# Moving one product and one subtraction per attention unit from GpSimd to VectorE

## The reference, cut to what matters

```python
xn = layernorm(x)                        # x: (8, 1024, 512), 8 images
q, k, v = (xn @ W.T + b, split in 16 heads of 32)
scores = where(tile_mask, q @ k.T / sqrt(32), -1e30)   # tile_mask: i % 256 >= j % 256
attn = softmax(scores) @ v
s = attn @ Wo.T + bo
g = silu(clip(xn @ sign(weights).T * scale + bias, -100, 100))
out = x + s * g
```

## Time and profile before

| | before |
|---|---|
| median of 3 runs | 1699.39 us (1696.45 to 1701.87) |
| profiled execution | 1697.66 us, span 1695.8 us |
| mean granted TensorE clock | 0.987 of full |
| TensorE busy | 1603.3 us |
| VectorE busy | 1237.8 us |
| ScalarE busy | 1203.0 us |
| GpSimd busy | 1157.7 us |

### The profile page before, as it was taken

The page is one execution under the profiler, slowest core; times in us unless marked ns, Lnnn a source line. Parts: engine busy times, 40 slices in busy tenths (PEclk is TensorE's granted clock), DMA queues, the critical chain, the costliest instruction groups (busy, mean ns, idle before and its releaser), DMA issues.

```text
span 1695.8 us, 34086 instructions
## 1 busy us (share of the span) xinstructions
PE 1603.3 (95%) x11812; PEld 681.8 (40%) x11812; DVE 1237.8 (73%) x1886; ACT 1203.0 (71%) x3057; POOL 1157.7 (68%) x1156
## 2 busy tenths in 40 slices
PE   8987999989999999998999989999999989999977
PEld 3432344433444344443444434443344434444423
DVE  7776676876767776787776967778676787667763
ACT  3475877767877777677776777866777767777752
POOL 0267657786677767775688765788657786677787
PEclk9998999999999999999999999999999999999999
DMA  7312312333124322244122532234312323222111
GB/s 208 119 39 69 76 45 58 99 78 89 48 55 100 91 62 52 70 106 85 42 58 76 118 72 51 56 80 105 85 43 64 97 74 64 51 64 70 50 53 50
DMA packets 182952, 125.97 MB, mean 74 GB/s; under 512 B 104734, under 2 KB 157214, under 8 KB 182332
## 3 DMA queue, kind: packets, MB, share of 16 engines
q1 hardware_dynamic: 182300, 123.40, 29.0%
q10 hardware_dynamic: 480, 0.39, 0.1%
HBM read 41.40 MB, written 17.02 MB: 34 GB/s over the span
## 4 chain that ended last, share of the span: by engine, by line
PE 61%; DVE 13%; issue 8%; ACT 7%; POOL 6%; SPq 3%; DMA 1%; POOLq 0%; DVEq 0%; ACTq 0%
PE pJ L568 24%; PE pO L791 11%; PE pJ L772 7%; POOL acc L1296 4%; DVE mx L1145 3%; SPq L1400 3%; PE pS L745 3%; PE pJ L768 2%; PE pJ L660 2%; ACT PT L893 2%; PE pJ L664 2%; PE pJ L661 2%; ACT pS L913 2%; PE pJ L711 2%; DVE acc L1173 2%
## 5 line engine op out<-in xcount | busy, mean ns | idle before, releaser
L893 ACT ACTIVATE PT<-pJ 128x512 f32<-128x512 f32 (+1 forms) x1080 | 608.6, 577 | 345.4 <-PE pJ L772 330.7
L1296 POOL TENSOR_TENSOR acc<-acc,PT 128x512 f32<-128x512 f32 (+1 forms) x640 | 779.5, 1256 | 24.0 <-PE pO L791 23.9
L772 PE MATMUL pJ<-QK 97*128 97x512 f16 (+3 forms) x1280 | 383.7, 319 | 7.5 <-ACT acc L893 6.6
L1145 DVE TENSOR_REDUCE mx<-pS 128x3 f32<-128x1536 f32 (+3 forms) x264 | 377.0, 1439 | 0.0
L1129 DVE TENSOR_REDUCE mx<-pS 128x1 f32<-128x384 f32 (+3 forms) x330 | 207.0, 633 | 100.7 <-PE pS L728 99.2
L1141 DVE TENSOR_REDUCE mx<-pJ 128x1 f32<-128x512 f32 (+3 forms) x264 | 151.4, 584 | 175.3 <-PE pJ L745 118.4
L791 PE MATMUL pO<-PT,V 128*32 128x512 f32 (+2 forms) x2800 | 259.4, 483 | 2.6 <-ACT PT L893 2.6
L913 ACT ACTIVATE pS<-pS,a 128x128 f32<-128x128 f32 (+1 forms) x480 | 245.8, 514 | 1.2
L568 PE MATMUL pJ<-xT,wh_q 128*128 128x512 f16 x512 | 194.0, 389 | 2.2 <-DVE xT L1107 1.8
L568 PE MATMUL pJ<-xT,wh_k 128*128 128x512 f16 x512 | 193.7, 381 | 2.0 <-DVE U L1240 2.0
L568 PE MATMUL pJ<-wh_v,xT 128*128 128x512 f16 x512 | 190.1, 380 | 1.3 <-DVE sg L1117 1.3
(11 more groups left out here) (172 smaller groups left out, 2759.4 us busy)
## 6 DMA issues: line engine op xcount, KB each, us to landing
QK<-sg SPq DMA_DIRECT2D x762, 64.0 KB, 2.0
xs<-in_x SPq DMA_DIRECT2D x60, 256.0 KB, 3.2
xr<-in_x SPq DMA_DIRECT2D x58, 256.0 KB, 3.1
out<-xr SPq DMA_DIRECT2D x58, 256.0 KB, 2.5
QK<-aT SPq DMA_DIRECT2D x256, 1.0 KB, 1.7
QK<-in_x SPq DMA_DIRECT2D x8, 256.0 KB, 3.8
rq<-moved SPq DMA_DIRECT2D x120, 2.0 KB, 1.8
QK<-in_mqk SPq DMA_DIRECT2D x2, 512.0 KB, 9.3
```

The lines of the kernel that those rows point to most:

```text
L772: ins = e.matmul(slot[:, to:to + 512 - q0], k4[0:97, j, kc], q4[0:97, j, q0:512], start=True, stop=True)
L893: e.activation(probabilities_at(i), bank("t", i)[:, 0:cols], ACT.Exp, scale=SS).then_inc(s_p, 1)
L1145: e.tensor_reduce(mx[:, par, part, :].rearrange("p (j q) -> p j q", q=4)[:, 0:3, qi], pS[:, :, c0:c0 + w], AX.X, ALU.max).then_inc(s_m0, 1)
L1296: e.tensor_tensor(a, a, PT[:, RING_AT[i] % NPT, 0:width * len(heads)].rearrange("p (j q) -> p j q", j=len(heads)), ALU.add).then_inc(s_ap, 1)
```

## The change

The product of odd units and the subtraction of all units but the last are issued by VectorE and no longer by GpSimd. The operands, the semaphores, the waits and the nominal times are the same; the two generators are handed to VectorE's in_time.

```diff
@@ vector: behind outputs() @@
+            def normalise_outputs():
+                for n in range(1, NU - 1, 2):
+                    yield past("sm", n) + TM["out"][2]
+                    ln.wait_ge(s_R, n + 1)
+                    ln.wait_ge(*outputs_taken(n))
+                    e.tensor_tensor(On[n % 2][:, :], On[n % 2][:, :], R[:, :], ALU.mult).then_inc(s_on, 1)
+            def low_outputs():
+                for n in range(NU - 1):
+                    gn, qs = divmod(n, NQS)
+                    s, cs = gn % NSLOT, slice(qs * 512, qs * 512 + 512)
+                    yield past("sm", n) + TM["hi"][1][1] if n in ADD_AT else at_pv(n, 3) + TM["hi"][1][0]
+                    ln.wait_ge(s_oh, n + 1)
+                    e.tensor_tensor(Onl[:, s, cs], On[n % 2][:, :], Onh[:, s, cs], ALU.subtract).then_inc(s_ol, 1)
...
-                    first_layer_norm(), layer_norm(), split_x(), take_xt(), stage_qk(), gates(), outputs(), last_outputs(), results(), last_results())
+                    first_layer_norm(), layer_norm(), split_x(), take_xt(), stage_qk(), gates(), outputs(), normalise_outputs(), low_outputs(), last_outputs(), results(), last_results())
@@ gpsimd @@
-            def normalise():
...
-            def low_outputs():
...
-            in_time(additions(), first_layer_norm(), layer_norm(), normalise(), low_outputs(), gates(), results())
+            in_time(additions(), first_layer_norm(), layer_norm(), gates(), results())
```

## The result

The changed kernel takes 1704.69 us (median of 9 runs, 1702.52 to 1708.08), the kernel before, run beside it, 1699.28 (9 runs, 1692.04 to 1702.03). The ratio is 1.0039 with a 95% interval of 1.0021 to 1.0056: slower by 6.6 us if the ratio is taken of 1699.28, by 5.4 by the medians. The forecast was 1706.0, slower. The profiled execution took 1702.68 us, its span is 1700.8.

What follows compares the result with a forecast made beforehand. TensorE was taken as the bound, with VectorE deciding at 955 to 976 us in each image. 6.0 + 0.5 + 2.0 - 0.4 - 1.0 = +7.1 us gave 1706.5 against the median, forecast 1706, range 1696 to 1718.

Steps and rivals of the forecast that it cites:

- the 0.76 us piece: TensorE idle ahead of L745 at 977.22, released by VectorE's maxima L1145; expected to grow by about 1 us.
- the pair: Subtractions of units 33 and 34, and their likes per image, landing ahead of VectorE's L1141 at 955.16.
- (a): Subtraction pairs 35/36, 37/38 and 39/40 land in VectorE idle time, such as 2.06 us ahead of L1141 at 1006.14: hidden.
- (b): Subtractions 33/34 entering VectorE's full stretch at 955 us: 1.0 us per image, 6.0 in six; last image 0.5.
- The holding: VectorE's two-input subtractions blocked by GpSimd's L1319 beside them: 0.4 us taken for each, between 0 and 1.07.
- The saving: L1232 at 951.99 shortens without GpSimd's subtraction beside it, so the pair begins up to 0.66 us earlier; 0.5 taken.
- (c): Products landing between VectorE's row-score maxima: 0.3 us per image for all four, 2.0 us over seven.
- (d): First image: subtraction 2 costs 0.9 us ahead of L1117; additions until 137.34 end 1.27 sooner; net -0.4 us.
- (e): GpSimd relieved elsewhere, where additions behind its subtractions mostly waited for TensorE anyway: -1.0 us for the whole kernel.
- GpSimd was the bound: Rival: shorter GpSimd queues finish the clamp sooner, so ScalarE's gate stops delaying exponentials: -12 us, 1687; chance 0.13.
- Held in full: Rival: both subtractions wait 1.07 us each, lower clock in more images: 2.8 us per image, +17.9, 1717; chance 0.08.
- Hidden: Rival: the subtractions at 955 us are never held and the 0.66 us is won in full: 1699; chance 0.29.

Runs made afterwards that it cites:

- run with the odd subtraction alone: Changed kernel with the even subtraction of each pair (seven) back on GpSimd, the odd one on VectorE: 1.0017 against the kernel before, +2.9 us.
- run with the pair given back: Changed kernel with the 14 subtractions of units 33, 34 and their likes, first image excepted, back on GpSimd: 0.9996 against the kernel before, -0.7 us.
- run with the pair alone: Kernel before with only the 14 subtractions of units 33, 34 and their likes on VectorE: 1.0042 against the kernel before, +7.1 us.
- the products alone: Kernel before with only the 31 products of the odd units on VectorE, all subtractions on GpSimd: 0.9991 against the kernel before, -1.5 us.
- the last version: Changed kernel with the pairs' and the first seven units' subtractions on GpSimd, the rest and all products on VectorE: 0.9987 against the kernel before, -2.2 us.
- the run in which the gate waits for the pair: Changed kernel with GpSimd's gate-bias addition beside each pair (seven) waiting until both subtractions are done: 1.0003 against the kernel before, +0.5 us.
- the even kernel: Changed kernel with the odd subtraction of each pair (seven) back on GpSimd, the even one on VectorE: 1.0034 against the kernel before, +5.8 us.

## Why the prediction was right, point by point

**What bounds the kernel.** Right in that VectorE decides at 955 to 976: behind the first image every other step that all kernels with the moved work share is under 0.3 us, and these go both ways. Wrong in where TensorE pays: not 22 us later at the 0.76 us piece, which grew by 0.09, but at the first L745 behind the pair, 1.15 us of idle time where there was none. That piece does pass on a delay that comes late enough, as the run with the odd subtraction alone shows (0.76 to 1.02).

**(a), the other pairs.** Right. In the run with the pair given back they are all on VectorE, with the products, and the time is that of the kernel before. In the changed kernel the subtractions L1222 waited for ScalarE 24 times, 1.2 us at most.

**(b), the pair.** Right in place and mechanism, and by luck right in size: the sum of 1.0 us per image came out at 1.00 at once and 1.09 some 20 us later, 6.5 us in six images for the 6.0 predicted. The run with the pair alone, +7.1 (4.6 to 9.7), agrees. But two of its terms were mis-sized, against each other. The holding was 0.8 us in the sum; it is 2.70 - 1.20 = 1.5. The saving was 0.5; L1232's successor L1248 fell from 1.34 to 0.69, and L1099 from 0.85 to 0.68 as well, together 0.8. So 2.70 - 0.51 - 0.65 - 0.17 = 1.37. Of this 1.20 is seen between the starts of the gate's product and of the result's first step (951.99 to 957.75, 953.11 to 960.07 now); the ends of records overlap the next starts. And TensorE made up 0.2 us of its own step right behind it, which the sum had no term for. The last image's 0.5 us was nothing: its pair takes 2.28 us (1565.47 to 1567.75), yet no step of TensorE stands behind it.

The size of the holding can be worked out from the changed kernel's rows. GpSimd's addition started at 954.68 and ended at 956.32; the first subtraction started at 955.11, and 0.6 us of its own work behind 956.32 make 956.9: its record (1.76 us) ends at 956.87. The clamp, 0.61 us long when free, started at 956.41 and took 0.94, to 957.35; the second subtraction ends 0.5 us later. GpSimd's addition had itself been held behind L1099 (1.64 for 1.28). So each waits for all that is left of the other's. The Trainium skill ("SBUF — State Buffer", section "Who interferes with whom") states this rule, and the trace agrees with it in size, not only in kind: 1.76 and 1.09 us for 0.69. The 0.4 us for each subtraction, taken from the mean of L1099, was the term that was too small. A mean over 56 places says how often a neighbour is there, not what it costs where it always is.

**(c), the products.** 2.0 us were predicted, and nothing of it shows. With the first image's gain the sum was +0.7; measured -1.5 (-3.9 to +0.8), which by itself would still allow it. The trace tells more: from 183 us on TensorE's delay doesn't grow (-0.4), and no place has a step in all the kernels that move the products. What was left over from VectorE's idle time was covered.

**(d), the first image.** The gain is there and smaller than said. Without GpSimd's product of unit 1, TensorE's wait at 137 us falls from 4.32 us (4.25 in the second profile of the kernel before) to 3.73, and to 3.49 with the products alone: 0.5 to 0.8 us for 1.27. The loss lay elsewhere than said. Subtraction 0 is held (1.13 us at 96.20), the one-input instruction behind it (L1003) takes 2.29 us where it took 1.66, and both delay L1117 and then TensorE's first L768, which has 1.4 us of idle time ahead of it in all nine profiles that have subtraction 0 on VectorE and none in the five others. The timeline of TensorE in the changed kernel:

```profile
102.46 0.23 PE L768 MATMUL pJ<-QK 128*128 128x128 f16 x1 [1.42 <-DVE sg L1117]
...
135.73 1.94 PE L711 MATMUL pJ<-V,ones 128*32 128x512 f32 x8 [3.73 <-POOL V L1312]
```

The net stays open, but it leans against the -0.4. Executions of one kernel differ by 3 us at 183 us. Still, the two kernels that move the products and leave subtraction 0 on GpSimd (the products alone, and the last version) are 6.5 and 5.6 us ahead of the first profile of the kernel before at that point, and the nine profiles with subtraction 0 on VectorE lie between 2.5 us ahead and 0.1 behind. By the times it isn't shown: putting the first seven units back gave 0.9987 for 0.9996, intervals that overlap.

**(e), GpSimd's relief.** The 1.0 us can't be seen by itself. The run with the pair given back (-0.7 us, from -2.5 to +1.0) has (a), (c), (d) and (e) together; by the prediction's terms these were +0.6.

**The rivals.** "GpSimd was the bound" fell with the table of waits: ScalarE's wait for the clamp stayed, and the additions waited for TensorE instead. "Held in full" had the holding about as far off on the other side (2.14 us for 1.5), and its lower clock isn't shown: the two profiles of the kernel before have it at two and two of the six images' ends, those of the changed kernel at two and four. "Hidden" would have been right without GpSimd's gate addition beside the pair, as the run in which the gate waits for the pair showed.

So the forecast came out near for a sum whose parts moved against each other: (b) 0.5 us too low, with a holding too small by 0.7 inside it, (c) some 2 us and the last image 0.5 too high, (d) probably too low.

## What to carry to other kernels

Work moved from GpSimd to VectorE is free or costly by where each piece lands, and what decides is the neighbour: 80 of 94 instructions cost nothing that the runs can tell, 14 cost 6.5 us by the trace and 7 by the ratios. Where a VectorE instruction with two SBUF inputs meets a GpSimd instruction at every repeat, charge it with all that is left of that instruction, and not with a mean; where VectorE is full there, order the two with a wait or keep one on GpSimd. Taking one of a pair out of a list sorted by nominal times can put the other somewhere else: look at its new neighbours and at every condition of its wait.

## What the runs showed that was not expected

- The holding goes both ways and chains: subtraction 1.76 and 1.09 us for 0.69, addition 1.64 for 1.28, clamp (one input) 0.94 for 0.61.
- A wait added to GpSimd made the changed kernel 6.1 us faster; GpSimd stood idle 3.76 us there instead of 1.89, and TensorE shows no step for it.
- Profiles of one kernel differ in where TensorE's clock falls: the even kernel had a granted clock of 0.81 (so a part of each stretch at 1.2 GHz) at six of six image ends once and at three of six the next time; the spans were 1706.8 and 1699.6 us. A difference of one or two us between two single profiles proves nothing here; a step at the same place in every image does.
